# Inverse transform of a spectral layer: products of eight channels and 256 columns, and a second product that crosses two PSUM banks

## What is computed

```python
def spectral_conv(x, w1, w2):
    x_ft = jnp.fft.rfft2(x)
    out_ft = jnp.zeros((b, w1.shape[1], h, w // 2 + 1), dtype=x_ft.dtype)
    out_ft = out_ft.at[:, :, :M1, :M2].set(jnp.einsum('bixy,ioxy->boxy', x_ft[:, :, :M1, :M2], w1))
    out_ft = out_ft.at[:, :, -M1:, :M2].set(jnp.einsum('bixy,ioxy->boxy', x_ft[:, :, -M1:, :M2], w2))
    return jnp.fft.irfft2(out_ft, s=(h, w))
...
for i in range(LAYERS):
    x1 = spectral_conv(h, w1, w2)
    x2 = jnp.einsum('bchw,oc->bohw', h, conv_w[i]) + conv_b[i][None, :, None, None]
    h = x1 + x2
    h = jnp.transpose(h, (0, 2, 3, 1))
    h = layer_norm(h, ln_g[i], ln_b[i])
    if i < LAYERS - 1:
        h = gelu(h)
```

## Time and profile before

| | |
|---|---|
| time, median of 3 runs | 7909.72 us (7907.23 to 7939.83) |
| time of the profiled execution | 7906.27 us |
| its span, first to last instruction | 7904.4 us |
| mean granted TensorE clock | 0.922 |
| busy: TensorE, ScalarE, VectorE, GpSimd | 86%, 64%, 62%, 54% of the span |
| DMA, mean over the span | 106 GB/s |

### The profile page before, as it was taken

One profiled execution on the slowest core, in us unless ns is written; L12 is line 12 of the kernel. 1 busy time (PEld: TensorE's weight loads), 2 busy tenths in 40 slices (PEclk: granted clock), 3 DMA queues, 4 the chain that ended last, 5 costly groups with the idle time before them and its releaser, 6 DMA issues. The chain is left out here.

```text
span 7904.4 us, 141712 instructions
## 1 busy us (share of the span) xinstructions
PE 6788.2 (86%) x45682; PEld 4620.4 (58%) x45682; DVE 4865.3 (62%) x7585; ACT 5032.1 (64%) x8721; POOL 4262.9 (54%) x1540
## 2 busy tenths in 40 slices
PE   7888789999799999799998899999999477777777
PEld 4555577777677777577776544444444255444555
DVE  7888657777467777477776333333333566777774
ACT  7888567778477777477777477777777233333332
POOL 7888457777267777177776144444444433333330
PEclk9999899999899999899999999999999687788888
DMA  2222344444444444444444411111111322333330
GB/s 84 94 98 94 129 157 158 159 158 155 162 144 159 154 156 156 153 155 158 152 159 138 140 50 45 49 50 44 50 47 41 99 67 68 69 69 69 69 68 3
DMA packets 597044, 835.29 MB, mean 106 GB/s; under 512 B 451944, under 2 KB 493032, under 8 KB 531304
## 3 DMA queue, kind: packets, MB, share of 16 engines
q1 hardware_dynamic: 596968, 834.27, 33.9%
HBM read 477.54 MB, written 356.58 MB: 106 GB/s over the span
## 5 line engine op out<-in xcount | busy, mean ns | idle before, releaser
L859 POOL TENSOR_TENSOR sb_rstd<-sb_var,sb_minus_half 128x16 f32<-128x16 f32 x1280 | 3690.0, 2900 | 2440.3 <-DVE sb_var L591 1219.3
L598 DVE TENSOR_TENSOR sb_unit<-H,sb_rstd 128x512 f32<-128x512 f32 x768 | 527.3, 687 | 517.1 <-POOL sb_rstd L859 511.7
L555 ACT ACTIVATE sb_pix<-sb_unit 128x512 f32<-128x512 f32 x768 | 827.7, 1078 | 0.0
L505 PEld LDWEIGHTS M<-sb_table,sb_pix 128*128 128x128 f32 x6144 | 712.1, 194 | 144.3 <-ACT sb_pix L555 125.1
L478 PE MATMUL H<-sb_conv_block,sb_act_in 128*128 128x128 f32 x6144 | 777.7, 280 | 0.0
L551 ACT ACTIVATE sb_act_px<-sb_unit 128x512 f32<-128x512 f32 x768 | 485.9, 633 | 451.0 <-DVE sb_unit L604 450.9
L478 PEld LDWEIGHTS H<-sb_conv_block,sb_act_in 128*128 128x128 f32 x6144 | 724.3, 194 | 38.2 <-issue 23.9
L505 PE MATMUL M<-sb_table,sb_pix 128*128 128x52 f32 x6144 | 737.0, 279 | 0.0
L591 DVE TENSOR_REDUCE sb_var<-sb_square 128x16 f32<-128x528 f32 x768 | 502.5, 696 | 236.4 <-ACT sb_square L544 236.4
L822 DVE COPY sb_act_out<-TC 128x512 f32<-128x512 f32 x256 | 177.0, 691 | 644.3 <-PE TC L672 644.3
L1812 ACT ACTIVATE blk_silu<-bank 114x260 f32<-114x260 f32 x384 | 148.7, 387 | 638.4 <-PE bank L1598 635.8
(11 more groups left out here) (273 smaller groups left out, 13588.2 us busy)
## 6 DMA issues: line engine op xcount, KB each, us to landing
act_scratch<-sb_act_out SPq DMA_DIRECT2D x256, 1024.0 KB, 3.9
sb_act_in<-act_scratch SPq DMA_DIRECT2D x256, 1024.0 KB, 5.3
spectrum_in<-sb_f_sb SPq DMA_DIRECT2D x512, 78.0 KB, 1.8
sb_x_in<-spectrum_in SPq DMA_DIRECT2D x48, 832.0 KB, 4.3
spectrum_out<-sb_y_sb SPq DMA_DIRECT2D x48, 832.0 KB, 4.6
sb_z_in<-spectrum_out SPq DMA_DIRECT2D x512, 78.0 KB, 5.1
blk_rows_b<-scan_rows SPq DMA_DIRECT2D x128, 260.0 KB, 7.2
blk_rows_bb<-scan_rows SPq DMA_DIRECT2D x128, 260.0 KB, 8.2
```

Of the source, the lines that this page charges most:

```text
L505: mm = e.matmul(M[u][:, 52 * g:52 * g + 52], pix[1 - p][:, at:at + 128], const("f1"), start=True, stop=True)
L555: e.activation(dst, unit[k % 2][:, :].rearrange("p (x c) -> p c x", c=16), gelu).then_inc(pix_ready, 1)
L598: e.tensor_tensor(rows, H[k][:, :].rearrange("p (y c) -> p y c", c=C), rstd[k][:, :].unsqueeze(2).to_broadcast([128, 16, C]), ALU.mult).th ...
L859: e.tensor_tensor(rstd[j][:, :], var[j][:, :], minus_half[:, :], ALU.pow).then_inc(rstd_ready, 1)
```

## The change

The ky step takes two channel groups (eight channels) as one stationary matrix of 116 columns, 52 for each group and 12 columns of zeros between them, and the whole table of 256 columns as moving operand. `z_in` is laid out with 64 columns for each group for that, and is set to zero once at the start. Four products replace sixteen. The row halves of `M[u]` and `v_sb` now hold even and odd channel groups, and each half has all 64 pixel rows.

So a chunk needs both row halves in the kx step: two products of 256 columns in place of one of 512. Each writes runs of four channels and leaves out the next four. Two products that run side by side from the two row halves may not write one bank, so the work crosses: first chunk j from the lower half with chunk j+1 from the upper, then, after a wait on TensorE's own semaphore `crossed`, the other way round. `to_channels` is moved between the two.

```diff
-        z_in = [sb(f"z_in{p}", [4 * B24, 2 * 8 * T26]) for p in range(2)]
+        z_in = [sb(f"z_in{p}", [4 * B24, 8 * 64]) for p in range(2)]
...
+        crossed = sem("first_halves_done")
...
-                e.dma_start(z_in[p][:, :].rearrange("q (g i m) -> q i g m", g=8, i=2)[:, i],
+                e.dma_start(z_in[p][:, :].rearrange("q (g w) -> q g w", g=8)[:, :, T26 * i:T26 * i + T26],
                             y_d[n * 2 + i].rearrange("q (g m) -> q g m", g=8)).then_inc(zl[p], 16)
...
-                gb = const("gb").rearrange("q (h t n) -> q t h n", h=2, t=2)
                 for u in range(2):
-                    for g in range(4):
-                        z = z_in[p][:, 52 * (4 * u + g):52 * (4 * u + g) + 52]
-                        for t in range(2):
-                            mm = e.matmul(M[u][64 * t:64 * t + 52, 128 * g:128 * g + 128], z, gb[:, t], start=True,
-                                          stop=True, skip_group_check=True)
+                    for g in range(2):
+                        at = 128 * (2 * u + g)
+                        mm = e.matmul(M[u][0:116, 256 * g:256 * g + 256], z_in[p][:, at:at + 116], const("gb"),
+                                      start=True, stop=True, skip_group_check=True)
                     mm.then_inc(a_done, 1)
...
-            def inverse_y(j):
+            def inverse_y(j, r, last):
+
+                e.matmul(H[j][:, :].rearrange("p (s r c) -> p s r c", r=2, c=4)[:, :, r, :],
+                         const("ga")[64 * r:64 * r + 52, :], v_sb[64 * r:64 * r + 52, 256 * j:256 * j + 256],
+                         start=False, stop=last, skip_group_check=True).then_inc(h_ready if last else crossed, 1)
+
+            def first_halves(j):
 
                 if j == 0:
                     e.wait_ge(v_ready, 2 * it + 2)
-                at = 64 * (j % 2)
-                e.matmul(H[j][:, :], const("ga")[at:at + 52, :], v_sb[at:at + 52, CH * (j // 2):CH * (j // 2) + CH],
-                         start=False, stop=True, skip_group_check=True).then_inc(h_ready, 1)
+                inverse_y(j, 0, False)
+                inverse_y(j + 1, 1, False)
+
+            def second_halves(j):
+
+                e.wait_ge(crossed, 4 * (it - pairs) + j + 2)
+                inverse_y(j, 1, True)
+                inverse_y(j + 1, 0, True)
...
                 if front and j % 2 == 0:
                     conv(j)
                     conv(j + 1)
+                    first_halves(j)
                 if three:
                     to_channels(*three)
                 if front and j % 2 == 0:
-                    inverse_y(j)
-                    inverse_y(j + 1)
+                    second_halves(j)
...
-                    v = v_sb[:, :].rearrange("r (y g c) -> r g y c", g=8, c=4)[:, 4 * u:4 * u + 4]
-                    e.activation(v, M[u][0:116, :].rearrange("r (g y c) -> r g y c", g=4, c=4),
+                    v = v_sb[:, :].rearrange("r (y g c) -> r g y c", g=4, c=4)[:, 2 * u:2 * u + 2]
+                    e.activation(v, M[u][0:116, :].rearrange("r (g y c) -> r g y c", g=2, c=4),
                                  ACT.Copy).then_inc(v_ready, 1)
...
+            for p in range(2):
+                e.memset(z_in[p][:, :], 0.0)
```

More of the change, by code:

```diff
@@ L639, in inverse_x @@
                     e.wait_ge(v_ready, 2 * it + 1)
[L640 to L644, removed]
-                                      stop=True, skip_group_check=True)
+                for g in range(2):
+                    at = 128 * (2 * u + g)
+                    mm = e.matmul(H[2][0:116, 256 * g:256 * g + 256], z_in[p][:, at:at + 116], const("gb"),
+                                  start=True, stop=True, skip_group_check=True)
                 mm.then_inc(a_done, 1)
@@ L658, in conv, with inverse_y, first_halves, second_halves @@
                              conv_block[:, :], start=(u == 0), stop=False, skip_group_check=True)
-            def inverse_y(j):
+            def inverse_y(j, r, last):
+                e.matmul(H[j % 2][:, :].rearrange("p (s r c) -> p s r c", r=2, c=4)[:, :, r, :],
+                         const("ga")[64 * r:64 * r + 52, :], v_sb[64 * r:64 * r + 52, 256 * j:256 * j + 256],
+                         start=False, stop=last, skip_group_check=True).then_inc(h_ready if last else crossed, 1)
+            def first_halves(j):
                 if j == 0:
                     e.wait_ge(v_ready, 2 * it + 2)
-                at = 64 * (j % 2)
-                e.matmul(H[j % 2][:, :], const("ga")[at:at + 52, :], v_sb[at:at + 52, CH * (j // 2):CH * (j // 2) + CH],
-                         start=False, stop=True, skip_group_check=True).then_inc(h_ready, 1)
+                inverse_y(j, 0, False)
+                inverse_y(j + 1, 1, False)
+            def second_halves(j):
+                e.wait_ge(crossed, 4 * (it - pairs) + j + 2)
+                inverse_y(j, 1, True)
+                inverse_y(j + 1, 0, True)
             def to_channels(c, k):
@@ L722, in pe_last @@
                 conv(1)
+            if front:
+                first_halves(0)
             if back:
@@ L725, in pe_last @@
             if front:
-                inverse_y(0)
-                inverse_y(1)
+                second_halves(0)
             if back:
@@ L740, in pe_last @@
                 conv(3)
+                first_halves(2)
                 to_channels(g0, 0)
-                inverse_y(2)
-                inverse_y(3)
+                second_halves(2)
             if back:
@@ L755, in intermediate @@
                 e.wait_ge(a_done, 2 * it + u + 1)
-                v = v_sb[:, :].rearrange("r (y g c) -> r g y c", g=8, c=4)[:, 4 * u:4 * u + 4]
-                e.activation(v, H[2][0:116, :].rearrange("r (g y c) -> r g y c", g=4, c=4),
+                v = v_sb[:, :].rearrange("r (y g c) -> r g y c", g=4, c=4)[:, 2 * u:2 * u + 2]
+                e.activation(v, H[2][0:116, :].rearrange("r (g y c) -> r g y c", g=2, c=4),
                              ACT.Copy).then_inc(v_ready, 1)
```

## The result

The changed kernel takes 7961.46 us (median of 4 runs, 7950.52 to 7973.39), the kernel before 7909.99 us beside it (4 runs, 7907.23 to 7939.83): a ratio of 1.0066, with an interval of 1.0043 to 1.0089. It is 52 us slower; 118 were forecast. Taken once more among the experiments it gave 1.0065 (1.0046 to 1.0084).

What follows compares the result with a forecast made beforehand. TensorE was taken to bound the kernel, within a ring of engines in middle steps and with ScalarE in the last pass. 71 + 51 = 122 us on 7906 gave 8028 us; range 7895 to 8130, the forecast's own 7970 to 8090.

Steps and rivals of the forecast that it cites:

- The ring and the place of each kx run: Middle steps: dependency cycle of 15.16 us, only chunks 0, 1's kx run on it; last pass: both runs on it.
- The price of an entry and exit: kx step: going from full array to row halves and back costs 0.40 us more for each run.
- 71 + 51: Added time in us: middle steps 0.37 times 192, last steps 0.80 times 64.
- The ky step: Array streams just as long: 0.03 us shorter in a middle step, 0 in a last one.
- Strided output, crossing, own wait in the change's order at 0: kx step: four-column runs and the `crossed` wait, covered by transposes and shape change, add nothing.
- the own wait: TensorE's wait for `crossed` in the kx step: costed at 0; if uncovered, 0.2 us at most a run.
- rival C: Whole kernel: no measurable difference, second entry partly free or full clock more often; 7900 to 7945 us, chance 0.16.
- two thirds of the exits: kx step: case giving the forecast's own lower bound of 7970 us.
- Rival A: kx step: strided output slows passes, up to 8357 us, a quarter of that about 8100; chance 0.15.
- B: ky and kx steps: number of products, not columns, sets the time; faster, 7746 us, chance 0.06.
- C's first ground: kx run: the 0.30 us around it may belong to inputs or waits, so a second entry is partly free.

Runs made afterwards that it cites:

- split_second: Kernel before with only the kx run of chunks 2 and 3 in the middle passes split in two around the transposes: 7859.58 us, ratio 0.9933.
- split_first: Kernel before with only the kx run of chunks 0 and 1 in the middle passes split in two around the transposes: 7988.31 us, ratio 1.0104.
- ky_only: Kernel before with the new ky step and `z_in` layout alone, kx step unchanged (result not the inverse transform): 7918.15 us, ratio 1.0013.
- split_only: Kernel before with each kx product cut into two of 256 adjacent columns around the transposes, all passes, no strided output or crossing: 7985.79 us, ratio 1.0095.
- fill_before_384: Kernel before with a useless 384-column TensorE product in front of the `forward_y` wait in each middle step: 7876.93 us, ratio 0.9935.
- late_copies: Kernel before with an unused 128-column ScalarE copy in each middle step, ahead of the copies `forward_y` waits for: 7940.1 us, ratio 1.0013.

## Why the prediction was wrong in size

- **The ring and the place of each kx run**: right. Period +0.32 us (0.37 forecast), and the run of chunks 2 and 3 costs nothing in period (`split_second`). TensorE's added work went into the wait: 0.98 to 0.45 us (about 0.6 forecast). The text counted only the second run there; `split_second` alone leaves mostly 0.63 us, but `split_first` takes off 0.17 too, to 0.81.
- **The price of an entry and exit**: 0.35 to 0.36 us, and 0.40 was taken. That is 0.05 x (192 + 128) = 16 us of the error, nearly all of the steps' own share: 71 + 51 became 61 + 47. The 0.30 us read from the rows were right; the 0.10 for the weight load behind the run were too much. The trace of the kernel before has the four transposes there, in ns (shortest/median/longest):

```profile
L493 PE MATMUL TC<-sb_table,sb_act_px x4: 272/272/328, 1709.8 to 1710.2; 128*128 128x128 f32 x4
```

  The first is 0.06 us longer than the others, and 0.30 + 0.06 is what was measured.
- **The ky step**: right, -0.03 us in the middle (`ky_only`), +0.02 in the last pass, where 0 was taken.
- **Strided output, crossing, own wait in the change's order at 0**: right (`split_only`). That the own wait costs 0.2 us at most when uncovered: too low, the second pair behind it costs 0.37 us. None of this enters the sum.
- **The step that failed**: the sum kept TensorE's clock in the middle passes as it was, with no reason given. It stood in rival C instead, as the whole of a case ("can give back ... 58 us", 0.16), and not as a term of the forecast. Yet the text itself derived the condition for it, a wait of 0.98 us in each middle step that goes to about 0.6. 55 us came back of the 70 that the falls cost (windows 0.97 before, 0.99 and 1.00 after), and that is most of the miss: 122 - 14 - 55 - 11 + 2 = 44. `fill_before_384` and `split_second` show the mechanism without the change.
- **Between the passes**: 11 us shorter, not forecast, and open (below).

Of the things by which the text said it would be wrong, two happened: the clock moved, and an entry cost 0.05 us less. The signs in the steps came out near (15.48 for 15.53 us, a last step +0.73 for +0.8). That 7961 us lie close to the forecast's lower bound of 7970 is no merit of that case, "two thirds of the exits": the exits cost nearly nine tenths, and the clock did the rest. Rival A (slow strided passes) is refuted by strided runs as long as contiguous ones, B (the number of products) by a ky step of 1.82 us for 1.85, and C's first ground, an entry that is partly free, by the 0.35 us; its second, the clock, was true beside the forecast.

## What to carry to other kernels

Where the windows show a clock under 1.00 on a kernel with no long pauses, look at what stands ahead of the slowed rows: if it is a short wait in each step, work added to TensorE beside the ring may pay for itself. Cutting a row-tiled run in two around a full-array run cost about 0.35 us here, and putting the second pair of products behind a wait for the first 0.37, so neither order rescued the split; count it only where the run is on the ring. Price the clock as a term of the sum whenever a change lengthens or shortens a wait of the engine that it drives, since a rival can be true beside the forecast.

## What the runs showed of the hardware

- With a wait of 0.9 to 1.0 us once in a step of 15.16 us, behind the 52-column products of `forward_x` and four transposes, the clock fell 40 times in 192 steps, 29 of them in or just behind the wait, at some 1.7 us each. With 0.45 to 0.64 us there (the changed kernel, `split_second`) or with the gap filled (0.24 to 0.66 us left) 5 to 8 falls remain, and only three of them, in `split_second`, come behind the wait. The fastest kernels were the kernel before with 192 useless columns in front of the wait (0.9929) and `split_second` (0.9933).
- The falls depend on when the steps come, too: with the wait at 1.07 to 1.18 us (`late_copies`) 12 and 11 steps in a row fell, and then none for hundreds of microseconds. What locks them together wasn't tried.
- Every kernel with the new ky step and layout of `z_in` has 159.6 to 161.3 us between the last ky row of one middle pass and the first of the next, every other 163.2 to 167.9 us. `ky_only` shows that it comes with that part. Most of it lies in the mixing, whose code no kernel changes: from the first to the last product between the last `forward_y` of a pass and the next ky step it takes 104.5 to 106.1 us with the new part and 107.9 to 112.1 without. Why stays open.
- The first ky row of the program starts between 1036.7 and 1073.9 us in the profiled executions, whatever the kernel, and TensorE waits there for the image loads (43 us in all from 400 to 700 us in the kernel before). Differences of some 20 us between two kernels mean little for this reason without several runs.
